# A post-norm transformer block: x of later batches turned by a DMA out of DRAM, two factors of the FP4 rounding folded into other instructions, and the turns of sums and context moved right behind the values

## The reference

```
x = layernorm(x + attention(x, w_qkv))            # 16 heads of 32, softmax, scores / sqrt(512)
x = layernorm(x + down(silu(gate(x)) * up(x)))    # all three linear layers in FP4
# FP4: for each block of 16 along the last axis, both operands
scale = max(max(abs(block)) / 6, 1e-12)
q     = nearest of (0, .5, 1, 1.5, 2, 3, 4, 6) to abs(block / scale), with the sign, times scale
```

## Time and profile before

| what | us |
|---|---|
| median of 3 runs (lowest, highest) | 3762.01 (3759.7, 3764.09) |
| the profiled execution | 3760.89 |
| its span, first to last instruction | 3759.1 |

### The profile page before, as it was taken

The page is one execution under the profiler, slowest core; times in us unless marked ns, Lnnn a source line. Parts: engine busy times, 40 slices in busy tenths (PEclk is TensorE's granted clock), DMA queues, the critical chain, the costliest instruction groups (busy, mean ns, idle before and its releaser), DMA issues.

```text
span 3759.1 us, 58354 instructions
## 1 busy us (share of the span) xinstructions
PE 3570.2 (95%) x21140; PEld 1582.8 (42%) x21322; DVE 3085.2 (82%) x4843; ACT 1739.6 (46%) x3072; POOL 2464.8 (66%) x1602
## 2 busy tenths in 40 slices
PE   3799999999999999999999999999999999999898
PEld 2344444344444344343443434444444344444244
DVE  9877898788977789778887789877898778977688
ACT  3466424564246632565226652366424663256522
POOL 2189645885469844798448974488645995469844
PEclk9899999999999999999999999999999999999999
DMA  5211232012321133101331122301222112311032
GB/s 182 87 29 35 66 67 68 19 44 71 69 52 32 38 79 69 49 26 33 87 73 40 32 59 66 72 25 35 73 65 63 27 39 74 67 45 32 1 74 64
DMA packets 354863, 209.39 MB, mean 56 GB/s; under 512 B 279696, under 2 KB 306320, under 8 KB 354448
## 3 DMA queue, kind: packets, MB, share of 16 engines
q1 hardware_dynamic: 354576, 205.65, 21.5%
HBM read 72.09 MB, written 19.66 MB: 24 GB/s over the span
## 4 chain that ended last, share of the span: by engine, by line
PE 72%; DVE 12%; issue 5%; POOL 3%; ACT 2%; DMA 1%; SPq 0%; DVEq 0%; POOLq 0%; ACTq 0%
PE SC L1708 18%; PE CT L1672 10%; PE R L717 8%; DVE mx L627 8%; PE SC L1657 7%; PE R L697 7%; PE CT L1730 6%; PE R L1708 6%; PE R L1730 5%; PE R L707 3%; PE R L729 2%; POOL wd L1252 2%; DMA split<-split 1%; ACT arena L1390 1%; DVE split L621 1%
## 5 line engine op out<-in xcount | busy, mean ns | idle before, releaser
L627 DVE TENSOR_REDUCE mx<-R 128x1 f32<-128x512 f32 x2048 | 1292.8, 683 | 342.9 <-PE R L717 338.3
L1390 ACT ACTIVATE arena<-SC 128x512 f32<-128x512 f32 x1364 | 753.8, 604 | 356.9 <-PE SC L1657 319.8
L1708 PE MATMUL SC<-wgu,split 128*128 128x512 f16 (+1 forms) x3456 | 708.8, 363 | 8.9 <-DMA split<-split 8.9
L1252 POOL TENSOR_TENSOR wd<-wd,arena 128x1024 f32<-128x1024 f32 x224 | 534.1, 2413 | 74.9 <-DVE wd L1514 69.2
L1708 PEld LDWEIGHTS SC<-wgu,split 128*128 128x128 f16 x3456 | 336.9, 98 | 364.9 <-DMA split<-split 19.8
L1282 POOL TENSOR_TENSOR arena<-arena,sc_h 128x512 f32<-128x512 bf16 (+2 forms) x144 | 178.4, 1253 | 465.1 <-DVE arena L550 465.1
L1390 ACT ACTIVATE wd<-SC 128x512 f32<-128x512 f32 x684 | 385.8, 604 | 182.4 <-PE SC L1657 168.6
L697 PE MATMUL R<-xT,wqkv 128*128 128x512 bf16 x1411 | 374.3, 380 | 26.0 <-DVE xT L614 13.0
L717 PE MATMUL R<-ks_even,qs_even 96*128 96x512 bf16 x1024 | 374.3, 384 | 20.0 <-DVE mx L627 10.2
L1657 PE MATMUL SC<-arena 98*128 98x512 bf16 x1024 | 372.9, 382 | 19.2 <-ACT arena L1390 7.5
L717 PE MATMUL R<-arena 96*128 96x512 bf16 x1024 | 374.0, 382 | 13.2 <-DVE xT L614 6.9
(11 more groups left out here) (152 smaller groups left out, 5272.8 us busy)
## 6 DMA issues: line engine op xcount, KB each, us to landing
x<-n_L_attn_embeddings_dram SPq DMA_DIRECT2D x120, 256.0 KB, 3.2
wd<-wd_kept SPq DMA_DIRECT2D x32, 512.0 KB, 4.3
out_dram<-x SPq DMA_DIRECT2D x64, 256.0 KB, 3.4
ks_even<-split SPq DMA_DIRECT2D x192, 64.0 KB, 2.0
qs_even<-split SPq DMA_DIRECT2D x384, 32.0 KB, 1.9
arena<-split SPq DMA_DIRECT2D x192, 64.0 KB, 2.0
arena<-split SPq DMA_DIRECT2D x384, 32.0 KB, 1.9
wd<-wd_kept SPq DMA_DIRECT2D x16, 384.0 KB, 5.4
```

The source lines that it names most:

```text
L627: nc.vector.reduce_max(mx[:, j:j + 1], ring_of(ring, job)[:, :], AX_X).then_inc(max_done, 1)
L1252: nc.gpsimd.tensor_tensor(acc[u % 2][i], acc[u % 2][i], probs_of(s)[:, hs, :], ALU.add).then_inc(pool_sum, 1)
L1390: nc.scalar.activation(probs_of(s)[:, hd, :], SC[e % SLOTS][:, :], ACT.Exp, scale=SCALE).then_inc(exp_done, 1)
L1708: last = nc.tensor.matmul(GU[kk % 2][which][:, 0:w], xhT[i % 2][:, part_x * KH + k, :], wgu[:, part_w * KH + k, which * I + first:which * ...
```

## The change

Four edits, and the buffers that they need.

1. `xT` of batches 2 to 7 no longer comes from PE. In the FFN stage of batch b (b up to 5), x of batch b + 2 is loaded tile by tile into `x_ahead`, ACT writes its high part (`high_ahead`), POOL its low part (`low_ahead`), and SP stores both to a tensor `x_split` in DRAM. In unit 5 of batch b + 1, once the last projection that reads the old `xT` is done, SP issues eight transposing DMAs from `x_split` into `xT`. The jobs "xT" and the loads of x in the attention stage stay only in batch 0 (for batch 1). ACT's first exponential of a batch also waits until the stores are done, since `x_ahead` and `x_halves` lie where the exponentials go. In POOL's FFN loop `low_x` is moved ahead of `inverse_deviation("out", ...)`.
2. `pool_sums`: POOL leaves one more tile to PE in units 5 and 6 of batches 1 to 7; before, only in the last batch.
3. `quantise`: the multiplication by `BELOW` (L536) and that of the scale by the gain (L538) are gone; the factor of the scale is in L534, and L544 becomes a scalar_tensor_tensor that multiplies by `BELOW` too. The same in the weight stage, where L999 goes as well.
4. In `unit_jobs`, place 3 of steps 1 to 7: the turns ("sumT", "ctx") and "xT" now stand ahead of the maximum's matmul, not behind it.

```
 def pool_sums(u):
-    return POOL_SUMS[u % UNITS] - (1 if u in range(UNITS * B - 3, UNITS * B - 1) else 0)
+    return POOL_SUMS[u % UNITS] - (1 if u >= UNITS and u % UNITS in (UNITS - 3, UNITS - 2) else 0)
...
-                  if b < B - 1 or not for_next(kind, a)] for place in places)
+                  if (b < B - 1 or not for_next(kind, a)) and (b == 0 or kind != "xT")] for place in places)
...
-    return of_batch(b, ([], m[0:1] + q[0:1], m[1:2] + total, neg + m[2:3] + other, m[3:4] + q[1:2], m[4:5] + q[2:] + m[5:]))
+    return of_batch(b, ([], m[0:1] + q[0:1], m[1:2] + total, neg + other + m[2:3], m[3:4] + q[1:2], m[4:5] + q[2:] + m[5:]))
...
-            link(nc.vector.tensor_scalar(scale, am, 1.0 / 6.0, 1e-12, ALU.mult, ALU.max))
+            link(nc.vector.tensor_scalar(scale, am, gain_ / 6.0, gain_ * 1e-12, ALU.mult, ALU.max))
             link(nc.vector.reciprocal(iv, scale))
-            link(nc.vector.tensor_scalar(iv, iv, BELOW, None, ALU.mult))
-            if gain_ is not None:
-                link(nc.vector.tensor_scalar(scale, scale, gain_, None, ALU.mult))
...
-            link(nc.vector.tensor_tensor(blocks_of(z), blocks_of(src), spread(iv, width // BLK), ALU.mult))
+            link(nc.vector.scalar_tensor_tensor(blocks_of(z), blocks_of(src), factor, spread(iv, width // BLK),
+                                                ALU.mult, ALU.mult))
...
+                        if u == UNITS - 3 and 0 < b < B - 1:
+                            sp.wait_ge(ring_full, ring.full(("proj", GROUPS * (b + 1) - 1, PROJ_JOBS - 1)))
+                            sp.wait_ge(ahead_stored, 16 * TILES * b)
+                            for t in range(TILES):
+                                sp.dma_start_transpose(xT_f[:, :, t * P:(t + 1) * P],
+                                                       x_split[t, :, :]).then_inc(xT_loaded[2 * t // TILES], 16)
...
+                    def load_ahead(i):
...
+                        if i >= 1:
+                            sp.wait_ge(ahead_hi, TILES * b + i)
+                            sp.wait_ge(ahead_lo, TILES * b + i)
+                        sp.dma_start(x_ahead, x_in[b + 2, :, :].rearrange("(p t) n -> p t n", t=TILES)[:, i, :]).then_inc(
+                            ahead_loaded, 16)
+
+                    def store_ahead(i):
...
+                        sp.wait_ge(ahead_lo, TILES * b + i + 1)
+                        sp.dma_start(x_split[i, :, :], x_halves).then_inc(ahead_stored, 16)
...
                     for i in range(TILES):
                         if 1 <= i < TILES - 1:
                             scale_x(at + i + 1)
+                        if 1 <= i < TILES - 1:
+                            low_x(at + i + 1)
                         if 2 <= i < TILES - 1:
                             inverse_deviation("out", at + i - 2)
-                        if 1 <= i < TILES - 1:
-                            low_x(at + i + 1)
...
+                        if b < B - 2:
+                            low_ahead(at + i)
...
+                act.wait_ge(ahead_stored, 16 * TILES * min(s // STEPS, B - 2))
...
                         silu(i, 1)
                         if i == at:
                             h_high(i, 0)
+                        elif b < B - 2:
+                            high_ahead(i - 1)
```

The two new pieces of work on ACT and POOL, for each tile:

```
+                    nc.scalar.activation(x_halves[:, 0:H], x_ahead, ACT.Copy).then_inc(ahead_hi, 1)
+                    nc.gpsimd.tensor_tensor(x_halves[:, H:2 * H], x_ahead, x_halves[:, 0:H], ALU.subtract).then_inc(ahead_lo, 1)
```

More of the change, by code:

```diff
@@ L334, in post_ln_block @@
         xs = xn.bitcast(F16)
-        hs = spare.bitcast(BF16)
+        hs = spare[:, 0:I].bitcast(BF16)
+        x_ahead, x_halves = spare[:, I:I + H], pw_w
+        xT_f = xT[:, :, :, :].rearrange("p a k s -> p (a k) s")
+        x_split = nc.dram_tensor("x_split", [TILES, P, 2 * H], BF16, kind="Internal").ap()
         sg = sg_f.rearrange("p (b n) -> p b n", b=2)
@@ L463, in post_ln_block @@
         qh_done = sem("qh_done")
+        ahead_loaded = sem("ahead_loaded")
+        ahead_hi = sem("ahead_hi")
+        ahead_lo = sem("ahead_lo")
+        ahead_stored = sem("ahead_stored")
+        xT_loaded = [sem(f"xT_loaded{n}") for n in range(HALVES)]
         hs_hi = sem("hs_hi")
@@ L692, in do @@
                     if a % GROUPS == 0 and j <= 1 and first == 0:
-                        pe.wait_ge(xT_done, TILES * (a // GROUPS - 1) + TILES // 2 * (j + 1))
+                        nb = a // GROUPS - 1
+                        if nb == 0:
+                            pe.wait_ge(xT_done, TILES // 2 * (j + 1))
+                        else:
+                            pe.wait_ge(xT_loaded[j], 16 * TILES // 2 * nb)
                     c = which * H + a % GROUPS * P
@@ L965, in quantise_down @@
                     dve.wait_ge(w_loaded[n % len(raw)], 32 * (n // len(raw) + 1))
-                    quantise(link, src, src, w, None, w_sc[r % 2][:, 0:w // BLK], w_r[r % 2][:, 0:w], rh_done,
+                    quantise(link, src, src, w, 1.0, w_sc[r % 2][:, 0:w // BLK], w_r[r % 2][:, 0:w], rh_done,
                              lambda: dve.wait_ge(qh_done, r - 1) if r >= 2 else None, None,
@@ L973, in quantise_gate_up @@
                     dve.wait_ge(w_loaded[n % len(raw)], 32 * (n // len(raw) + 1))
-                    rounded_to_grid(link, src, src, 2 * H, inv_gu[:, first:first + GU_BLOCKS], w_r[r % 2][:, 0:2 * H], rh_done,
+                    rounded_to_grid(link, src, src, 2 * H, inv_gu[:, first:first + GU_BLOCKS], BELOW, w_r[r % 2][:, 0:2 * H], rh_done,
                                     lambda: rounded_free(r), pw_w, grid)
@@ L1126, in units @@
                             sp.wait_ge(stored[par], 16 * TILES // 2 * b)
[L1127 to L1129 removed]
+                    if b == 0:
+                        load_x(x_next, 0)
+                        load_x(x_next, 1)
                     def load_turn(t):
@@ L1136, in units @@
                         g, used = GROUPS * b + u // 2 + 1, GROUP * TILES * (UNITS * b + u)
-                        turns = [t + 2 for t, (turn_u, _) in enumerate(X_TURNS) if turn_u == u and t + 2 < TILES and b < B - 1]
+                        turns = [t + 2 for t, (turn_u, _) in enumerate(X_TURNS) if turn_u == u and t + 2 < TILES and b == 0]
                         if u == UNITS - 2:
@@ L1194, in turn_h @@
                                                    hs[:, 2 * first * P:2 * (first + k) * P]).then_inc(hT_loaded[n], 16)
+                    def load_ahead(i):
+                        if b >= B - 2:
+                            return
+                        if i >= 1:
[4 more added lines that the diff above has]
+                    def store_ahead(i):
+                        if b >= B - 2:
+                            return
+                        sp.wait_ge(ahead_lo, TILES * b + i + 1)
+                        sp.dma_start(x_split[i, :, :], x_halves).then_inc(ahead_stored, 16)
                     turn_x(0)
@@ L1198, in tiles @@
                     load_down(b, 0)
+                    if 0 < b < B - 1:
+                        for loaded in xT_loaded:
+                            sp.wait_ge(loaded, 16 * TILES // 2 * b)
+                    load_ahead(0)
                     turn_x(1)
@@ L1209, in tiles @@
                                 store(i - 2)
+                        store_ahead(i - 1)
+                        load_ahead(i)
                     turn_h(TILES - 1)
-                    for i in range(TILES - 3, TILES):
+                    store(TILES - 3)
+                    store_ahead(TILES - 1)
+                    for i in range(TILES - 2, TILES):
                         store(i)
@@ L1220, in _ @@
                 sp.wait_ge(x_kept, 16 * TILES * (B - 1))
+                sp.wait_ge(ahead_stored, 16 * TILES * (B - 2))
+                for loaded in xT_loaded:
+                    sp.wait_ge(loaded, 16 * TILES // 2 * (B - 2))
                 for par in range(2):
@@ L1458, in tiles @@
                     silu(last, 1)
+                    if b < B - 2:
+                        high_ahead(last - 1)
                     h_high(last, 0)
@@ L1462, in tiles @@
                     h_high(last, 2)
+                    if b < B - 2:
+                        high_ahead(last)
                     second_norm(last - 2)
@@ L1572, in quantise_h @@
                     n = slice(cols.start // BLK, cols.stop // BLK)
-                    quantise(link, h[:, cols], h[:, cols], cols.stop - cols.start, None, sc_h[:, n],
+                    quantise(link, h[:, cols], h[:, cols], cols.stop - cols.start, 1.0, sc_h[:, n],
                              r_h[:, cols], rh_done, scale_free)
```

14 lines of the change are left out of this document (8 added, 6 removed).

## The result

The changed kernel takes 3723.06 us (median of 4 runs, 3719.49 to 3724.08) where the kernel before, beside it, takes 3761.47 us: a ratio of 0.9896, with a 95% interval of 0.9883 to 0.9908, or 38.4 us less. The forecast was 3726 us. The profiled execution took 3722.25 us with a span of 3720.5.

What follows compares the result with a forecast made beforehand. PE, busy 95% of the span, was taken as the bound. Terms of -33.6 (xT and sums), -2.4 and -0.4 (quantise) and 0 (order) made -36.4 us from 3760.9: 3724.5, forecast as 3726, range 3707 to 3750.

Steps and rivals of the forecast that it cites:

- Unit 5: Unit 5, batches 1 to 6: without PE's turns of x and their waits, 34.7 us becomes 30.2, a gain of 4.5.
- Units 6 and 7: Batches 1 to 6: longer PE sums cost 0.88 us each, removed waits return 1.4 and 1.43; -0.55 each.
- what is late next: Unit 5's next limit once the turns go: neighbouring units suggested below 29.5 or 31.8 us; 30.2 was taken.
- Cost 0: FFN stage: ACT's copy and POOL's 1.16 us subtraction fit into POOL's 3.30 us wait; without that cover, 1.8 us a tile.
- rival C: FFN stage: POOL's new subtraction delays h or x, 0.9 us a tile in 48 tiles, +43, so 3769 us; chance 0.04.
- FFN stages: Folded quantise in the eight FFN stages: DVE is not the limit, so only 0.3 us a batch, -2.4 us in all.
- Quantise in the weight stage: Weight stage, DVE without idle time: dearer products +1.7 us, removed instructions -2.1, net -0.4; ends -2.1 and +3.4.
- Order: Attention: turns ahead of the maximum's matmul change PE's 19.9 us of bank waits; ends -19.9 and +10.6, taken as 0.
- the order's doing: Sign of being wrong: batch 0 and the last batch changed by more than 2 us, blamed on the moved turns.
- B: Weight stage and FFN rounding of h: the new scalar_tensor_tensor takes double time, total +16, 3778 us; chance 0.06.
- A: Late attention units are held by POOL and ACT, not PE, so less is gained: 3748 us; chance 0.12.
- D: Units 5 to 7 reach PE's own work, 8 us a batch, and the order gives some: 3706 us; chance 0.10.

Runs made afterwards that it cites:

- undo_pool: The changed kernel with POOL's sums in units 5 and 6 of batches 1 to 6 as before: 3743.27 us, ratio 0.9958 to the kernel before.
- undo_quant: The changed kernel with the old quantise, its two factors instructions of their own again: 3749.56 us, ratio 0.9973 to the kernel before.
- undo_order: The changed kernel with the turns of sums and context behind the maximum's matmul again: 3717.8 us, ratio 0.9889 to the kernel before.
- only_order: The kernel before with only the turns moved ahead of the maximum's matmul: 3764.69 us, ratio 1.0012.
- order_pool: The changed kernel with the old order and POOL's shorter sums in units 2 and 4 too: 3719.98 us, ratio 0.9890 to the kernel before.
- narrow_low: The changed kernel with old quantise and POOL's new subtraction 32 columns wide instead of 512 (timing only): 3726.21 us, ratio 0.9909 to the kernel before.
- only_pool: The kernel before with only POOL's shorter sums in units 5 and 6 of batches 1 to 6: 3762.13 us, ratio 1.0006.
- only_quant: The kernel before with only the two quantise factors folded in: 3754.55 us, ratio 0.9989.

## Why the prediction was right, and which of its steps were not

The time (3726 against 3723.06) and most stage lengths came out. Two of its costs of zero did not, and that the total came out so close is in part luck: two terms, each wrong by about 23 us, cancel.

**Unit 5: right.** 30.2 us forecast, 29.90 measured; -4.76 a batch for -4.5. No wait for `xT` is left. The largest one is 0.8 us ahead of the sum, until 1231.33; the view names a DVE maximum, but POOL's last addition of unit 4 ends at 1231.18, the same 0.15 us before as in the earlier trace rows, so by that reading it is POOL again.

**Units 6 and 7: right in size, half right in reason.** Unit 6 34.08 (about 34.1 forecast), unit 7 24.17 (-0.58 for -0.55). But I put the worth of POOL's shorter sums at a removed wait of 1.43 us in unit 7. The missing piece is undo_pool: without them unit 6 is 2.4 to 5.3 us longer once unit 5 is shorter, 2.4 for the wait and the rest at half clock behind it. The step "what is late next" was asked for unit 5 alone, and its answer was POOL in unit 6.

**Batches 1 to 6: -5.1 us each for -5.6.** The three late units give -5.97; in batch 1 half a microsecond of it goes back in unit 1 (+0.27) and units 2 to 4 (+0.25), in others to single units that are longer.

**"Cost 0" of the new work in the FFN stage: the cover named was the wrong one.** I looked at POOL's order and found 3.30 us of idle time for its new subtraction. POOL did have it. What the subtraction holds up is DVE, whose instructions on SBUF sit out POOL's, and by that the h of each tile: 3.9 us a stage, 23 us for six. That is rival C by another way, at 0.49 us a tile where I had priced it at 0.9. It does not show in the changed kernel because edit 3 takes two instructions out of DVE's chain. So edit 3 was worth 26.5 us here and 5.8 alone, where I had 2.8. The two mistakes, of about 23 us each, cancel, and nothing in the prediction foresaw that they would. The clue stood in the trace of before: L536 takes 993 ns on average at 32 columns, all of them outside the weight stage, and 188 at 48 columns in it, and I took it only as a small instruction.

**FFN stages: -5.9 measured for -2.4, but most of it is the clock.** I had booked 0.3 in each of the eight. In batches 0 to 6 the sum is -2.8, of which -2.4 is batch 3 with its spell of low clock before; the six others give -0.5 together. The last one, which has no added work, gives -3.1. The experiments split that: with the low clock at its start it takes 184.7 us with the old quantisation (undo_quant) and 183.2 with the new (undo_pool), without it 181.5 with the new (after, undo_order). So about 1.5 us are the shorter chain and 1.6 the clock.

**Quantise in the weight stage: -3.4 for -0.4.** The new instruction is no dearer than the old (1217 against 1218 ns); I had added 8%. Its end of -2.1 was the nearest one. The rest is POOL once more, and chance: the subtraction at 768 columns takes 0.96 us free and 3.73 held, and is held twice of four times before (L550, mean 2343 ns) and once after (L556, mean 1651), while at 640 columns one L549 is held that was not before (mean 1024 ns for 825). Over the profiled executions the stage takes 173.8 to 176.9 us with the old quantisation (six kernels, mean 175.5) and 171.2 to 173.9 with the new (seven, mean 172.5).

**Order: 0 forecast, a cost of 1 to 5 us measured**: only_order +4.3, undo_order -5.3 by medians and -2.6 by ratios, order_pool -1.3 beside the changed kernel. The wait that it was meant to shorten did shrink. Waits over the span, before in the earlier trace rows, now:

```profile
PEld R L749 <- DVE mx L633: 10.3, 17, 0.8
```

19.9 us became 10.3, and the time did not fall with it. The price shows in the units of every batch from 1 to 6: unit 1 is 0.27 us longer with the new order (31.54 against 31.27), units 2, 4 and 5 about 0.1 each, and unit 7 0.2 shorter. That this is the maximum a few turns later is what the edit suggests; no run shows it by itself. The measured cost lies within the ends given (-19.9 to +10.6).

**Last batch: +3.5 us, in no step of the forecast** except as its sign for "the order's doing". Nearly all is unit 6 (28.64 to 32.18). The clock explains it. Windows of the kernel after in that unit; in the first two PE waits 1.07 and 0.96 us (until 3474.41 and 3476.69) for ACT's exponential, where before it waited 0.98 and 1.19 at the same place with the clock at 1.00:

```profile
3472.00:3475.00 3.00, 1.85 (x8) 0.62 (x9) 2.37 (x4) 1.60 (x4) 3.00 (x2) 1.00 0.00 0
3475.00:3478.00 3.00, 2.04 (x9) 0.35 (x11) 1.62 (x3) 1.08 (x2) 0.95 (x1) 0.53 0.00 0
3478.00:3481.00 3.00, 3.00 (x16) 0.59 (x12) 2.73 (x3) 0.00 (x0) 0.00 (x0) 0.50 0.00 0
3481.00:3484.00 3.00, 3.00 (x23) 0.78 (x16) 0.22 (x1) 1.58 (x4) 1.39 (x1) 0.84 0.00 0
```

In the profiled executions this unit takes 28.6 to 29.6 us where its mean granted clock is 1.00 (before, undo_quant, narrow_low) and 31.3 to 32.7 where it is 0.89 to 0.95 (the ten others, among them only_pool, only_quant and only_order, which have one edit each). Why the same waits bring the clock down in some and not in others stays open. No single edit decides it, and with one profiled execution of each kernel it may as well differ between executions of the same one: those of the kernel before spread from 3755 to 3764 us at mean clocks of 0.990 to 0.996.

**Two signs of being right did not come:** the new product near 750 ns at 512 columns (mean 1473), and a last batch within 2 us (+3.5). The first is POOL's hold, the second the clock.

**The rivals.** B (the new instruction takes double time) is refuted: 1217 ns at 1024 columns, where double would be 2436, and 692 at 512 where POOL is idle. By the rule of the Trainium skill's Vector Engine (DVE) Microarchitecture Reference, section 7, it should have been slower; the trace does not agree. The mean of 1473 ns at 512 columns looks like it at first sight, but undo_quant and narrow_low show what it is: a plain tensor_tensor of that size is stretched too when POOL is busy (1194 ns) and not when it isn't (692). A's mechanism is real without edit 2, C's without edit 3. D (more gained) did not come.

## What to carry to other kernels

Read a DVE instruction's mean duration by form against the same form where POOL is idle: the surplus is time spent behind POOL, and an instruction added on POOL has to be priced on DVE's chain as well as in POOL's own order. When a stage is made shorter, ask again which engine still has to finish a fixed amount of work inside it, since that one's last step becomes the next wait, and here, behind a PE wait of some 3 us, the slower clock doubled the next values' time. Before two stages of two kernels are compared, compare their granted clocks: two of the differences above were the clock alone. Test edits together as well as alone: here the largest one lost 15 us alone and earns 38 with two small ones beside it.

## What the runs showed of the hardware

- A tensor_scalar of 32 columns on DVE takes 0.18 us where POOL is idle and 1.89 us in the row above, beside a POOL tensor_tensor of 1024 columns; 93 of 93 that start inside a POOL instruction end behind it (L536, kernel before). A reciprocal of the same size is not held (0.35 us in all 96). One such instruction more in each of 160 places costs 14 us of a kernel that PE bounds.
- scalar_tensor_tensor with two float32 sources in SBUF and a spread second source: 692 ns at 512 columns where POOL is idle, 1217 at 1024, 1625 at 1408, the same as tensor_tensor (692, 1218, 1626).
- A transposing DMA of 256 KB out of DRAM takes 1.31 us to issue and 3.9 us to land, against 1.23 and 2.7 within SBUF.
- PE's granted clock is 0.50 for at least 5.6 us behind a wait of 3.18 us (undo_pool, batch 1), and in the last batch of the changed kernel it is 0.50 to 0.53 behind two waits of about 1 us, which in the kernel before left it at 1.00.
